# Two-layer transformer on one core: in the mixture of experts, the experts' shares come by DMA from scratch memory instead of by a matmul

## The chip, the cores and the metric

The kernel runs on one core of one Trainium2 chip. The metric is the device time of one execution in microseconds (us). A core has five engines that run their own instruction streams and wait for one another on semaphores: PE (TensorE, the matrix engine; its weight loads are listed apart as PEld), DVE (VectorE), ACT (ScalarE), POOL (GpSimd) and SP, which here only issues DMAs. PE writes its results to PSUM, eight banks of 512 fp32 values for each of 128 partitions; DVE and ACT read and write PSUM and SBUF; POOL and the DMAs don't reach PSUM.

## The reference, cut to what matters

The program computes two transformer layers on 4096 tokens of width 256. The change touches only the last part, the mixture of experts of layer 1:

```python
probs = softmax(xf @ router_w + router_b)          # 64 experts
tw, ti = top_k(probs, 8);  tw = tw / sum(tw)
for e in experts:                                   # hidden width 64 each
    h = silu(xf @ W1[e] + B1[e]) @ W2[e] + B2[e]
    cw = sum(where(ti == e, tw, 0))                 # the expert's share of each token
    acc += cw[:, None] * h
shared = sum over 2 shared experts of silu(xf @ sw1 + sb1) @ sw2 + sb2   # hidden width 512 each
out = x + acc + shared
```

All 64 experts are computed for all tokens; a token's share of an expert is zero unless the expert is among its best 8. The share is multiplied into the expert's hidden layer, before the second product.

## The kernel before

`moe_blocks` works on 8 blocks of 512 tokens, with features on the partitions and tokens along the free axis. A block has 40 chunks of 128 hidden rows: chunks 0 to 7 are the shared experts, chunks 8 to 39 are 32 pairs of experts with 64 rows each. Every fp32 product is made of three matmuls of rounded halves (hi by hi, hi by lo, lo by hi; the helper `product3`, lines 67 to 69), so a chunk's first layer is 6 matmuls into `m_h` ("hidden") and its second layer 6 more that accumulate into `m_y` ("output"). PE's order is written out by hand: hidden(c), then output(c-2) (`LAG` is 2), then hidden(c+1), and so on. Between hidden(c) and output(c) the chunk passes through ACT and DVE:

- ACT, line 1939: Silu with bias, from `m_h` in PSUM to `m_h_full` in SBUF
- DVE, line 2042, expert chunks only: multiply by the share, which is in `m_c` in PSUM
- ACT, line 1945: round to `m_h_hi`
- DVE, line 2045: subtract, to `m_h_lo`

The shares come from the router. At the start of a block PE makes the logits (into `m_turn`), DVE and ACT make the softmax and the best 8 between chunks 0 and 6, PE transposes the 64 by 512 shares after chunk 7 (line 1911), and DVE cuts them into `cw`, 64 rows of hi parts above 64 rows of lo parts (lines 2030 and 2032). A row of `cw` is one expert, but a chunk needs the row of expert 2p on 64 partitions and that of expert 2p+1 on the other 64. PE spreads them: a matmul of `cw` with a 0/1 matrix `pick_pair` (line 1852), which POOL writes for each pair (line 1826). This matmul stands in PE's order right behind hidden(c), and waits for `cw` in the block's first expert chunk:

```python
project3(nc, h_ps[:, c % 2, :], w, ln.cut[0], cols).then_inc(h_done, 1)
if c >= SC:
    ...
    nc.tensor.matmul(c_ps[:, c % 2, :], pick_pair[...], cw[:, :], start=True, stop=True).then_inc(spread, 1)
```

Among the chunks lies other work: in chunks 12 to 22 the LayerNorm of the next block (PE's two sums, lines 143 and 150; ACT's square root with two table loads, line 185, ahead of chunk 18; DVE's reciprocal in two halves behind chunks 19 and 21, line 165, and its scaling behind 22, line 170). In block 0 the experts' weights are also split into hi and lo, one item in each of 18 chunks (ACT line 991, DVE line 996). Behind a block's chunk 2 PE transposes the finished block before it into `m_c` (line 1881) and ACT copies it out in two instructions (line 1951).

PSUM is full: `m_turn`, `m_h`, `m_c` and `m_y` have two banks each. `m_h_full`, `m_h_hi` and `m_h_lo` have a ring of three places.

Of the kernel before, what the change touches and what calls it, by code (L numbers as in the profile page):

```python
# [112 lines left out]
def count(events):  # L113


    return events + FIRST
# [1605 lines left out]
HEAD = 3  # L1722


def moe_blocks(nc, d, K, w1, w2, s1, s2, rw, items):
# [7 lines left out]
    with ExitStack() as ctx:  # L1733
# [4 lines left out]
        h_full = sb("m_h_full", [P, RING, TB], F32)  # L1738
        h = [sb(f"m_h_{p}", [P, RING, TB], F32R) for p in ("hi", "lo")]
        best, row_max, row_sum = sb("best", [P, TT, TOP], F32), sb("row_max", [P, TT], F32), sb("row_sum", [P, TT], F32)  # L1740
        cw = sb("cw", [P, TB], F32R)
        pick = sb("pick", [P, E], F32)
        pick_pair = sb("pick_pair", [P, 2, 2, EH], F32R)
# [3 lines left out]
        turn_ps, h_ps, c_ps, y_ps = (ps(n, [P, 2, TB]) for n in ("m_turn", "m_h", "m_c", "m_y"))  # L1747
        (bias_loaded, pick_set, b_cut, x_loaded, x_reloaded, logit_done, logit_ready, max_ready,
         cent_ready, exp_ready, best_ready, drop_ready, kept_ready, sum_ready, r_ready, cw_ready, cw_turned,
         cw_hi, cw_lo, h_done, spread, full_ready, hi_ready, lo_ready, h_free, x4_ready, out_turned,  # L1750
         out_ready, out_stored, kept_weights, picked, dve_passed, pe_passed, passed) = (
            sem(n) for n in (
                "bias_loaded", "pick", "b_cut", "x_loaded", "x_reloaded", "logit_done",
                "logit_ready", "max", "cent", "exp", "best", "drop", "kept", "sum", "r", "cw", "cw_turned",
                "cw_hi", "cw_lo", "h_done", "spread", "full", "hi", "lo", "h_free", "x4", "out_turned",
                "out_ready", "out_stored", "kept_weights", "picked", "dve_passed", "pe_passed",
                "pool_passed"))
        sp_passed = sem("sp_passed")
        ln = LayerNorm("ln4", nc, sb, sem, K["ones"], [x], x_loaded, turn_ps[:, 0, :], turn_ps[:, 1, :])

        logits, dropped = (ln.xc[:, k, 0:TT * E].rearrange("p (t e) -> p t e", t=TT) for k in range(2))
        b2_raw = h_full[:, 2, 0:D]
# [12 lines left out]
        def heads_and_tails(eng, head, tail):  # L1775

            head(0, False)
            tail(0, True)
            head(1, True)
            with eng.Fori(1, NB - 1) as i:  # L1780
                tail(i, True)
                head(i + 1, True)
            tail(NB - 1, False)

        sem.start()
        with nc.Block() as block:
# [25 lines left out]
            @block.gpsimd  # L1812
            def _(pool):

                nc.gpsimd.memset(pick[:, :], 0.0).then_inc(pick_set, 1)
                for n, base in enumerate((0, -E)):
                    pool.wait_ge(pick_set, count(n + 1))
                    nc.gpsimd.affine_select(out=pick[:, :], in_=pick[:, :], compare_op=ALU.not_equal,
                                            fill=1.0, base=base, pattern=[[-1, E]],
                                            channel_multiplier=1).then_inc(pick_set, 1)  # L1820
                pool.wait_ge(pick_set, count(3))
                with pool.Fori(0, NB) as i:
                    for p in range(PAIRS):
                        pool.wait_ge(spread, count(i * PAIRS + max(p - 1, 0)))
                        alone(pool, passed)
                        nc.gpsimd.tensor_copy(pick_pair[:, p % 2, :, :],
                                              pick[:, 2 * p:2 * p + 2].unsqueeze(2).to_broadcast([P, 2, EH])
                                              ).then_inc(picked, 1)
                        pool.wait_ge(picked, count(i * PAIRS + (p + 1)))

            @block.tensor
            def _(pe):
                def hidden(i, c):
                    pe.wait_ge(full_ready, count(i * C + max(c - 1, 0)))
# [8 lines left out]
                    project3(nc, h_ps[:, c % 2, :], w, ln.cut[0], cols).then_inc(h_done, 1)  # L1843
                    if c >= SC:
# [310 lines left out]
```

## Time and profile before

| what | value |
|---|---|
| median of 3 runs | 4845.29 us (4844.75 to 4852.0) |
| the profiled execution | 4846.32 us, of which the span from first to last instruction is 4844.7 us |
| mean granted TensorE clock | 0.962 of full speed |
| busy over the span | PE 93%, PEld 56%, DVE 75%, ACT 65%, POOL 11% |
| the mixture of experts | its first matmul starts at 3793.8 us; 8 blocks of about 126 us each |

A matmul's listed duration contains its way through the pipeline, and matmuls overlap: for the pace of PE, the distance between starts is to be read, not the duration. A number in brackets behind a row of the timeline is how long the engine sat idle ahead of it, and what ended that. In a line that groups instructions, the first numbers are the busy time and the mean of one.

### The profile page before, as it was taken

Reading aid. Unit: us, or ns where it says so; the run is one execution under the profiler, and the core shown is the slowest. Engines: PE = TensorE matmul, PEld = TensorE weight load, DVE = VectorE, ACT = ScalarE, POOL = GpSimd, SP = SyncE. Lnnn points to the kernel's source line nnn. Section 1 sums busy time; section 2 is a strip of 40 time slices with the busy share of each in tenths; the row PEclk is TensorE's granted clock in tenths of the full one; section 3 lists DMA queues with packets and bytes.
Section 4 is the critical chain, followed back from the end, with each engine's and each line's share of the span. In section 5 each row is a group of like instructions: output and inputs, shape, how many; then the busy total and the mean of one; then the engine's idle time right before and its main releaser. Section 6 shows DMA issues by size and latency. Waiting matters only on the chain. (4 is left out here: it accounts for less than half of the span.)

```text
span 4844.7 us, 107645 instructions
## 1 busy us (share of the span) xinstructions
PE 4509.8 (93%) x36227; PEld 2729.0 (56%) x36227; DVE 3645.8 (75%) x3699; ACT 3157.8 (65%) x5605; POOL 541.7 (11%) x1382
## 2 busy tenths in 40 slices
PE   6599999999999999999999969999885799999999
PEld 4344444444444444444444447777654478888887
DVE  4599999899999999999999956555355554444444
ACT  3158888788888888888888834444464454444444
POOL 4501111111111111111111100000000000000000
PEclk8789999999999999999999979999998899999999
DMA  5611110200202012012122220010001300000000
GB/s 174 190 29 21 24 28 18 34 18 18 34 18 34 19 21 35 18 31 65 39 56 45 44 88 28 25 35 9 27 17 48 123 14 9 13 13 13 13 4 14
DMA packets 217985, 182.41 MB, mean 38 GB/s; under 512 B 128032, under 2 KB 167632, under 8 KB 216448
## 3 DMA queue, kind: packets, MB, share of 16 engines
q1 hardware_dynamic: 201152, 167.99, 14.0%
q0 software_dynamic: 16384, 8.42, 0.7%
q8 instruction: 283, 4.64, 0.4%
q14 instruction: 166, 1.36, 0.1%
HBM read 120.47 MB, written 71.89 MB: 40 GB/s over the span
## 5 line engine op out<-in xcount | busy, mean ns | idle before, releaser
L894 DVE TENSOR_REDUCE PM<-A 128x2 f32<-128x1024 f32 x2092 | 2457.2, 1220 | 97.3 <-PE A L781 64.9
L871 ACT ACTIVATE PR<-SB 128x512 f32<-128x512 f32 x4100 | 2121.1, 603 | 367.2 <-PE SB L794 354.6
L814 PE MATMUL PV<-PR,VH 128*32 128x256 f32 x16384 | 1293.4, 387 | 3.5 <-issue 3.5
L781 PE MATMUL A<-QST,KA 48*128 48x512 f32 x4184 | 1196.4, 476 | 67.0 <-DMA QF<-QFD 40.8
L814 PEld LDWEIGHTS PV<-PR,VH 128*32 128x32 f32 x16384 | 433.2, 110 | 557.9 <-issue 367.0
L781 PEld LDWEIGHTS A<-QST,KA 48*128 48x128 f32 x4184 | 428.7, 187 | 525.1 <-issue 457.8
L794 PE MATMUL SB<-KST,QST 50*128 50x512 f32 x3075 | 689.8, 411 | 5.1 <-ACT PR L871 4.6
L794 PEld LDWEIGHTS SB<-KST,QST 50*128 50x128 f32 x3075 | 387.9, 187 | 213.3 <-ACT PR L871 209.3
L2045 DVE TENSOR_TENSOR m_h_lo<-m_h_full,m_h_hi 128x512 fp32r<-128x512 f32 x320 | 221.6, 693 | 276.5 <-ACT m_h_hi L1945 276.2
L802 PE MATMUL SB<-KF,QF 99*32 99x512 bf16 x4100 | 414.9, 384 | 1.2 <-ACT PR L871 1.2
L1939 ACT ACTIVATE m_h_full<-m_h,constants 128x512 f32<-128x512 f32 x320 | 219.6, 686 | 255.4 <-PE m_h L69 254.2
L1945 ACT CAST m_h_hi<-m_h_full 128x512 fp32r<-128x512 f32 x320 | 198.6, 621 | 249.9 <-DVE m_h_full L2042 247.9
L2042 DVE TENSOR_TENSOR m_h_full<-m_h_full,m_c 128x512 f32<-128x512 f32 x256 | 175.0, 684 | 217.8 <-ACT m_h_full L1939 190.3
L1247 DVE SCALAR_TENSOR_TENSOR chosen<-gate_out,h_ps 128x512 f32<-128x512 f32 x128 | 87.1, 681 | 182.1 <-PE h_ps L69 181.7
L953 POOL DMA_DIRECT2D NUM<-OS x256 | 126.7, 495 | 864.1 <-ACT OS L882 800.6
L1186 ACT ACTIVATE h_full<-chosen,constants 128x512 f32<-128x512 f32 x128 | 92.3, 721 | 198.4 <-DVE chosen L1247 198.4
L67 PE MATMUL m_h<-ln_hi,moe_w_hi 128*128 128x512 f32 x512 | 209.0, 408 | 0.0
L67 PE MATMUL m_y<-m_h_hi,moe_w_hi 128*128 128x512 f32 x512 | 201.5, 393 | 1.8 <-DVE m_h_lo L2045 1.8
L68 PE MATMUL m_h<-ln_lo,moe_w_hi 128*128 128x512 f32 x512 | 202.6, 396 | 0.0
L69 PE MATMUL m_h<-ln_hi,moe_w_lo 128*128 128x512 f32 x512 | 202.1, 395 | 0.0
L68 PE MATMUL m_y<-m_h_lo,moe_w_hi 128*128 128x512 f32 x512 | 202.0, 394 | 0.0
L69 PE MATMUL m_y<-m_h_hi,moe_w_lo 128*128 128x512 f32 x512 | 199.7, 390 | 0.0
(280 smaller groups left out, 5503.6 us busy)
## 6 DMA issues: line engine op xcount, KB each, us to landing
QST<-QS SPq DMA_DIRECT2D x54, 256.0 KB, 9.0
KA<-KAD SPq DMA_DIRECT2D x402, 32.0 KB, 1.8
KST<-KS SPq DMA_DIRECT2D x402, 32.0 KB, 1.9
QS<-parts SPq DMA_DIRECT2D x16, 512.0 KB, 5.6
KS<-parts SPq DMA_DIRECT2D x16, 512.0 KB, 4.7
KAD<-dealt SPq DMA_DIRECT2D x16, 512.0 KB, 3.3
m_x<-X3T SPq DMA_DIRECT2D x16, 512.0 KB, 3.8
moe_w_lo<-W SPq DMA_DIRECT2D x16, 512.0 KB, 10.0
```

The costliest lines, as they stand in the source:

```text
L67: nc.tensor.matmul(out, w[0], x[0], start=first, stop=False)
L68: nc.tensor.matmul(out, w[0], x[1], start=False, stop=False)
L69: return nc.tensor.matmul(out, w[1], x[0], start=False, stop=last)
L781: return nc.tensor.matmul(A[:, u % 2 * 2 + e, :], keys, QST[rows, slot, j * TB:(j + 1) * TB], start=True, stop=True)
L794: nc.tensor.matmul(SB[:, s_bank(v), :], QST[rows, slot, c * P:(c + 1) * P], KST[rows, nb % K_SLOTS, :], start=True, stop=True).then_inc(s_ ...
L802: mm = nc.tensor.matmul(SB[r * 2 * HD:(r + 1) * 2 * HD, s_bank(v), :], QF[0:FINE_ROWS, slot, at:at + 2 * HD], KF[0:FINE_ROWS, nb % K_SLOTS ...
L814: mm = nc.tensor.matmul(PV[at:at + 2 * HD, 0:HB], VH[:, slot, e, c, :], PR[:, (2 * c + e) % P_SLOTS, b * HB:(b + 1) * HB], start=(c == 0), ...
L871: nc.scalar.activation(PR[:, v % P_SLOTS, :], SB[:, s_bank(v), :], ACT.Exp, scale=SCALE).then_inc(s_free, 1)
L894: nc.vector.tensor_reduce(PM[:, par, :, i, j:j + 1], A[:, u % 2 * 2:u % 2 * 2 + 2, :], AX.X, ALU.max).then_inc(a_free, 1)
L1939: nc.scalar.activation(h_full[:, c % RING, :], h_ps[:, c % 2, :], ACT.Silu, bias=bias).then_inc(full_ready, 1)
L1945: nc.scalar.copy(h[0][:, c % RING, :], h_full[:, c % RING, :]).then_inc(hi_ready, 1)
L2045: nc.vector.tensor_tensor(h[1][:, c % RING, :], h_full[:, c % RING, :], h[0][:, c % RING, :].bitcast(F32), ALU.subtract).then_inc(lo_ready, 1)
```

## The change

The matmul of line 1852, `m_c`, `pick` and `pick_pair` go. DVE copies the transposed shares once more, as fp32, into `m_shares` in SBUF. POOL stores them to scratch memory (`CW`, 64 by 512, fp32, 128 KB), waits for that store, and then issues two DMAs for each pair: row 2p of `CW` to all of partitions 0 to 63 of a slot of `m_shares`, and row 2p+1 to partitions 64 to 127 (128 KB written each). There are three slots; the loads of pair p wait until DVE has multiplied pair p-3. DVE waits for a pair's two DMAs and multiplies.

The two banks of `m_c` are given out anew: `m_h` has three banks, and the transposes of the finished block have one, `m_out`, so these are done and copied out in two halves (behind chunk 2 and in chunk 3). ACT's Silu and DVE's multiplication now write their result back to `m_h` in PSUM, and the two splits read it there; `m_h_full` is gone. The router's steps on DVE and ACT, and PE's transposes of the shares, each come one chunk earlier. PE's wait for `cw` moves to the products with the second bias at the block's end.

```diff
             def _(pool):
-                nc.gpsimd.memset(pick[:, :], 0.0).then_inc(pick_set, 1)
...
                 with pool.Fori(0, NB) as i:
+                    pool.wait_ge(cw_full, count(i + 1))
+                    alone(pool, passed)
+                    pool.dma_start(d["CW"], shares[0:E, 0, :]).then_inc(shares_stored, 16)
+                    pool.wait_ge(shares_stored, i * 16 + 16)
+                    alone(pool, passed)
                     for p in range(PAIRS):
-                        pool.wait_ge(spread, count(i * PAIRS + max(p - 1, 0)))
-                        alone(pool, passed)
-                        nc.gpsimd.tensor_copy(pick_pair[:, p % 2, :, :],
...
+                        if p >= SHARE_SLOTS:
+                            pool.wait_ge(kept_ready, count(i * PAIRS + (p - SHARE_SLOTS + 1)))
+                            alone(pool, passed)
+                        for e in range(2):
+                            pool.dma_start(shares[e * EH:(e + 1) * EH, p % SHARE_SLOTS, :],
+                                           d["CW"][2 * p + e, :].partition_broadcast(EH)
+                                           ).then_inc(share_loaded[p % SHARE_SLOTS], 16)
...
                 def hidden(i, c):
-                    pe.wait_ge(full_ready, count(i * C + max(c - 1, 0)))
+                    pe.wait_ge(lo_ready, count(i * C + max(c - 2, 0)))
...
-                    project3(nc, h_ps[:, c % 2, :], w, ln.cut[0], cols).then_inc(h_done, 1)
-                    if c >= SC:
...
-                        nc.tensor.matmul(c_ps[:, c % 2, :],
...
+                    project3(nc, h_ps[:, c % RING, :], w, ln.cut[0], cols).then_inc(h_done, 1)
...
-                    nc.scalar.activation(h_full[:, c % RING, :], h_ps[:, c % 2, :], ACT.Silu,
+                    nc.scalar.activation(h_ps[:, c % RING, :], h_ps[:, c % RING, :], ACT.Silu,
                                          bias=bias).then_inc(full_ready, 1)
...
-                    nc.scalar.copy(h[0][:, c % RING, :], h_full[:, c % RING, :]).then_inc(hi_ready, 1)
+                    nc.scalar.copy(h[0][:, c % RING, :], h_ps[:, c % RING, :]).then_inc(hi_ready, 1)
...
                     elif step == "cut":
                         dve.wait_ge(cw_turned, count(i + 1))
+                        nc.vector.tensor_copy(shares[0:E, 0, :], turn_ps[0:E, 1, :]).then_inc(cw_full, 1)
...
-                        dve.wait_ge(spread, count(i * PAIRS + (c - SC + 1)))
-                        nc.vector.tensor_tensor(h_full[:, c % RING, :], h_full[:, c % RING, :], c_ps[:, c % 2, :],
+                        slot, turn = (c - SC) % SHARE_SLOTS, (c - SC) // SHARE_SLOTS
+                        turns = len(range(slot, PAIRS, SHARE_SLOTS))
+                        dve.wait_ge(share_loaded[slot], i * (32 * turns) + 32 * (turn + 1))
+                        nc.vector.tensor_tensor(h_ps[:, c % RING, :], h_ps[:, c % RING, :], shares[:, slot, :],
                                                 ALU.mult).then_inc(kept_ready, 1)
...
-                        router(i, {4: "best", 5: "drop", 6: "weights", 7: "cut"}.get(c))
+                        router(i, {3: "best", 4: "drop", 5: "weights", 6: "cut"}.get(c))
```

On PE, where the shared chunks end and the expert chunks begin in block 0, `m_y` being the second layer, `m_h` the first, and line 1911 the transposes of the shares:

```order
 L68 MATMUL m_y<-m_h_lo,moe_s_hi 128x512
 L69 MATMUL m_y<-m_h_hi,moe_s_lo 128x512
-L1911 MATMUL m_turn<-ident,ln_xc 64x128 x4
-L67 MATMUL m_h<-ln_hi,moe_w_hi 128x512
-L68 MATMUL m_h<-ln_lo,moe_w_hi 128x512
-L69 MATMUL m_h<-ln_hi,moe_w_lo 128x512
-L67 MATMUL m_h<-ln_hi,moe_w_hi 128x512
-L68 MATMUL m_h<-ln_lo,moe_w_hi 128x512
-L69 MATMUL m_h<-ln_hi,moe_w_lo 128x512
-L1852 MATMUL m_c<-cw,pick_pair 128x512
```

The transposes have moved up by one chunk (they stand ahead of hidden(7) now), and behind hidden(8), as behind each later expert chunk, the matmul of line 1852 is gone; the six of hidden stand there as before.

On DVE, at the same place of block 0, before (line 996 is a weight's split, lines 2020 and 2024 the router's step "weights", lines 2030 and 2032 the step "cut"):

```order
L2045 TENSOR_TENSOR m_h_lo<-m_h_full,m_h_hi 128x512
L2020 TENSOR_TENSOR ln_xc<-ln_xc 128x256
L2024 TENSOR_TENSOR ln_xc<-ln_xc,row_sum 128x256
L996 TENSOR_TENSOR moe_w_lo<-moe_w_lo,moe_w_hi 128x1024
L2045 TENSOR_TENSOR m_h_lo<-m_h_full,m_h_hi 128x512
L2030 CAST cw<-m_turn 64x512
L2032 TENSOR_TENSOR cw<-m_turn,cw 64x512
L2042 TENSOR_TENSOR m_h_full<-m_h_full,m_c 128x512
```

and now:

```order
L2020 TENSOR_TENSOR ln_xc<-ln_xc,row_sum 128x256
L2044 TENSOR_TENSOR m_h_lo<-m_h,m_h_hi 128x512
L2025 COPY m_shares<-m_turn 64x512
L2027 CAST cw<-m_turn 64x512
L2029 TENSOR_TENSOR cw<-m_turn,cw 64x512
L996 TENSOR_TENSOR moe_w_lo<-moe_w_lo,moe_w_hi 128x1024
L2044 TENSOR_TENSOR m_h_lo<-m_h,m_h_hi 128x512
L2041 TENSOR_TENSOR m_h<-m_h,m_shares 128x512
```

The copy to `m_shares` is ahead of the cut, and chunk 7's last step (the second line 2044) now lies between the cut and the first multiplication.

On POOL, the start of a block, where ahead of the change each row was a write of `pick_pair` (line 1826):

```order
L1817 ISA
L1820 DMA CW<-m_shares 64x512
L1821 ISA
L1828 DMA m_shares<-CW 64x512 x6
L1825 ISA
L1828 DMA m_shares<-CW 64x512 x2
```

The store is followed by the six loads of pairs 0 to 2 without a wait among them, and then by two loads for each further pair.

## Rows read from the trace of the kernel before

**Rows 1.** Busy time by stretch, one block of the mixture of experts (PE first)

```profile
core 0: us, PE busy (x) PEld busy (x) DVE busy (x) ACT busy (x) POOL busy (x), PEclk, DMA share, GB/s
4593.00:4716.00 123.00, 122.48 (x541) 98.45 (x540) 59.90 (x96) 57.14 (x85) 10.46 (x32) 1.00 0.04 13
```

**Rows 2.** Groups by line, the whole mixture of experts

```profile
L1852 PE MATMUL m_c<-cw,pick_pair 128*128 128x512 f32 x256 | 101.2, 395 | 4.6 <-DVE cw L2032 4.4 <-DVE m_h_full L2042 0.2
```

**Rows 3.** What PE waited for there: us in total, times, longest

```profile
PE m_c L1852 <- DVE cw L2032: 4.4, 8, 1.0
PE m_y L67 <- DVE m_h_lo L2045: 1.8, 3, 1.0
```

**Rows 4.** Timeline, the steady pace: the last two expert chunks of a block

```profile
4449.00 0.39 PE L1852 MATMUL m_c<-cw,pick_pair 128*128 128x512 f32 x1
...
4451.77 0.39 PE L69 MATMUL m_h<-ln_hi,moe_w_lo 128*128 128x512 f32 x1
4452.00 0.39 PE L1852 MATMUL m_c<-cw,pick_pair 128*128 128x512 f32 x1
4452.20 0.69 ACT L1939 ACTIVATE m_h_full<-m_h,constants 128x512 f32<-128x512 f32 x1 [0.85 <-PE m_h L69]
...
4453.01 0.69 DVE L2042 TENSOR_TENSOR m_h_full<-m_h_full,m_c 128x512 f32<-128x512 f32 x1 [0.94 <-ACT m_h_full L1939]
...
4453.73 0.62 ACT L1945 CAST m_h_hi<-m_h_full 128x512 fp32r<-128x512 f32 x1 [0.84 <-DVE m_h_full L2042]
...
4454.39 0.69 DVE L2045 TENSOR_TENSOR m_h_lo<-m_h_full,m_h_hi 128x512 fp32r<-128x512 f32 x1 [0.69 <-ACT m_h_hi L1945]
...
4455.93 0.39 PE L67 MATMUL m_y<-m_h_hi,moe_w_hi 128*128 128x512 f32 x1
```

**Rows 5.** Timeline, chunks 18 to 23 of a block, with the next block's LayerNorm

```profile
4515.85 1.28 ACT L185 ACT_TABLE_LOAD   x1
...
4516.26 0.39 PE L69 MATMUL m_h<-ln_hi,moe_w_lo 128*128 128x512 f32 x1
...
4519.15 0.69 ACT L1939 ACTIVATE m_h_full<-m_h,constants 128x512 f32<-128x512 f32 x1
...
4519.96 0.69 DVE L2042 TENSOR_TENSOR m_h_full<-m_h_full,m_c 128x512 f32<-128x512 f32 x1 [3.40 <-PE m_c L1852]
...
4534.35 0.68 DVE L2042 TENSOR_TENSOR m_h_full<-m_h_full,m_c 128x512 f32<-128x512 f32 x1
```

**Rows 6.** Group by line: the weights' splits on DVE in block 0

```profile
L996 DVE TENSOR_TENSOR moe_w_lo<-moe_w_lo,moe_w_hi 128x1024 fp32r<-128x1024 f32 x16 | 19.7, 1230 | 6.6 <-ACT moe_w_hi L991 6.6
```

**Rows 7.** Timeline, chunks 7 and 8 of a block, with the shares' way

```profile
4478.74 0.40 PE L69 MATMUL m_h<-ln_hi,moe_s_lo 128*128 128x512 f32 x1
...
4480.72 0.48 PE L67 MATMUL m_h<-ln_hi,moe_w_hi 128*128 128x512 f32 x1
...
4481.16 0.68 DVE L2030 CAST cw<-m_turn 64x512 fp32r<-64x512 f32 x1
...
4481.96 0.40 PE L69 MATMUL m_h<-ln_hi,moe_w_lo 128*128 128x512 f32 x1
...
4482.87 0.49 PE L1852 MATMUL m_c<-cw,pick_pair 128*128 128x512 f32 x1 [0.52 <-DVE cw L2032]
```

**Rows 8.** DMA issues by kind: count, KB each, median us from issue to landing

```profile
NUM<-OS POOLq DMA_DIRECT2D x256, 16.0 KB, 2.0
out<-ln_sq SPq DMA_DIRECT2D x8, 512.0 KB, 3.0
constants<-in_L_attn_b_qkv SPq DMA_DIRECT2D x1, 128.0 KB, 4.6
```

**Rows 9.** DMA rate in 0.1 us slices of 2546 to 2550 us

```profile
GB/s 0 0 0 0 0 0 0 0 0 103 164 225 185 195 123 113 10 0 0 20 0 0 0 72 51 31 21 0 0 82 0 0 0 0 0 0 0 0 0 0
```

**Rows 10.** Timeline of POOL, two of eight DMAs (16 partitions of 1 KB each)

```profile
2785.30 0.48 POOL L953 DMA_DIRECT2D NUM<-OS  x1
2785.78 0.48 POOL L953 DMA_DIRECT2D DEN<-OS  x1
```

**Rows 11.** Groups by line: the same two splits with a PSUM source

```profile
L287 ACT CAST wt_hi<-setup_ps 128x512 fp32r<-128x512 f32 x8 | 4.4, 593 | 10.0 <-PE setup_ps L268 9.9
L298 DVE TENSOR_TENSOR wt_lo<-setup_ps,wt_hi 128x512 fp32r<-128x512 f32 x8 | 5.1, 683 | 12.9 <-ACT wt_hi L287 12.9
```

More of the change, by code:

```diff
@@ L1906, in tail @@
                         output(i, c - LAG)
-                        if c == SC - 1:
+                        if finish and c == HEAD:
+                            turn_output(i - 1, 1)
+                        if c == SC - 2:
                             pe.wait_ge(cw_ready, count(i + 1))
@@ L1927, in _ @@
                 heads_and_tails(pe, head, tail)
-                turn_output(NB - 1)
+                for part in range(2):
+                    turn_output(NB - 1, part)
             @block.scalar
@@ L1944, in chunk, with copy_output @@
                         act.wait_ge(kept_ready, count(i * PAIRS + (c - SC + 1)))
-                    nc.scalar.copy(h[0][:, c % RING, :], h_full[:, c % RING, :]).then_inc(hi_ready, 1)
-                def copy_output(i):
-                    act.wait_ge(out_turned, count(i + 1))
-                    for t in range(2):
-                        nc.scalar.copy(out_tok[:, 2 * t:2 * t + 2, :],
-                                       c_ps[:, t, :].rearrange("p (a n) -> p a n", a=2)).then_inc(out_ready, 1)
+                    nc.scalar.copy(h[0][:, c % RING, :], h_ps[:, c % RING, :]).then_inc(hi_ready, 1)
+                def copy_output(i, part):
+                    act.wait_ge(out_turned, count(i * 2 + (part + 1)))
+                    nc.scalar.copy(out_tok[:, 2 * part:2 * part + 2, :],
+                                   out_ps[:, :].rearrange("p (a n) -> p a n", a=2)).then_inc(out_ready, 1)
                 def head(i, finish):
@@ L1957, in head, with tail @@
                     if finish:
[L1958 to L1960 removed]
+                        copy_output(i - 1, 0)
+                def tail(i, following, finish):
                     for c in range(HEAD, C):
[L1962 removed]
+                        if finish and c == HEAD + 1:
+                            copy_output(i - 1, 1)
+                        if c == HEAD:
                             act.wait_ge(cent_ready, count(i + 1))
@@ L1984, in _ @@
                 heads_and_tails(act, head, tail)
-                copy_output(NB - 1)
+                for part in range(2):
+                    copy_output(NB - 1, part)
             @block.vector
```

76 lines of the change are left out of this document (30 added, 46 removed).

## The prediction, made before the changed kernel was run

> **What bounds the kernel now.** I read the table of stretches first. One block of the mixture of experts takes some 123 us, and in it PE is busy for all but half a microsecond, at the full clock of 2.4 GHz (granted clock 1.00), while DVE and ACT are busy for half of it [rows 1]. What PE waited for in the whole part is small too: 4.4 us for the shares, once in each block, and 1.8 us for the split hidden layer [rows 3]. So this part is bound by the number of PE's instructions, and one matmul less in its stream should be worth its distance to the next. The timeline gives that distance: from the matmul of line 1852 in one chunk to that in the next are 3.00 us for 13 matmuls, 0.231 us each [rows 4] (the group's mean of 395 ns holds the pipeline as well [rows 2]).
>
> The second thing to read is how late the ACT and DVE steps may be. In a chunk without other work the last matmul of hidden starts at 4451.77, Silu 0.43 later, the multiplication 0.81 after that, the rounding 0.72, the subtraction 0.66, and it takes 0.69: the chunk is ready 3.31 us after the start of that matmul [rows 4]. PE comes back for it after output(c-2), hidden(c+1), output(c-1), hidden(c+2) and three matmuls of line 1852, 28 starts later: 6.47 us. The slack is 3.1 us, and it is what now hides everything that DVE and ACT do beside the chunks.
>
> **The matmuls that go.** There are 256 of line 1852 [rows 2], at 0.231 us: 59.2 us, if nothing takes their place.
>
> **The wait that goes.** In the first expert chunk PE starts its last matmul of hidden at 4481.96 and that of line 1852 only at 4482.87, 0.91 us later instead of 0.23: 0.68 us, of which 0.52 are shown as idle [rows 7]. With the same 0.16 us beside the idle time in all 8 blocks the 4.4 us [rows 3] become 5.7 us. The new reader of `cw`, the bias at the block's end, comes 80 us later and never waits.
>
> **The slack that shrinks.** The chunk's period falls to 12 × 0.231 = 2.77 us. PE comes back for a chunk after 25 starts, 5.77 us. The reads from PSUM change the two splits a little: rounding takes 593 ns from PSUM [rows 11] against 0.62, the subtraction 683 ns [rows 11] against 0.69. What it costs or gives to write the Silu and the product to PSUM no row shows, since nothing but PE writes there before. I bound it by what the source does, 0.03 us better or worse for each, take nothing, and get 3.27 us from matmul to ready chunk, and some 0.1 for the wake-up: 2.4 us of slack. The Trainium skill ("ScalarE: Activation LUTs", Step-by-step: what each stage is for) says that ACT writes faster to PSUM than to SBUF; by it the Silu would fall towards the lower bound and some of the stalls below would go. No run here shows it yet.
>
> Where is the slack used up? At chunk 18 ACT is held by two table loads and the square root from 4515.85, and its Silu starts at 4519.15. Now hidden(18) is complete in time for a start at 4516.26 + 0.43 = 4516.69, 2.46 us earlier [rows 5], inside the 3.1. With the new pace that matmul comes 0.23 us sooner, while ACT's work behind chunk 17 does not: 2.67 us late, over the slack by 0.27. From there to chunk 23 DVE has the reciprocal twice and the scaling as well: multiplication to multiplication 4519.96 to 4534.35, 14.39 us for 5 chunks [rows 5], 14.2 with the quicker splits. PE's five periods are 5 × 3.00 = 15.0 now, so the chain catches up; they will be 13.87, so it falls behind by another 0.33. PE is stalled by 0.27 + 0.33 = 0.6 us in each of the 6 blocks between the first and last: 3.6 us. Block 0 has the weights' splits in addition, 1.2 us of DVE each [rows 6]. From chunk 18 to 28 the chain needs 11 × 2.05 (its own minimum, 0.81 to the multiplication, 0.72 to the rounding and 0.52 until ACT takes the next Silu) + 7 × 1.2 for the splits there + 3.3 for the square root (4515.85 to 4519.15) + 4.1 for reciprocals and scaling (14.39 less 5 × 2.05 [rows 5]) = 38.4 us. PE needs 33.0 for 11 chunks now, and 38.4 - 33.0 - 3.1 = 2.3 is near the 1.8 us plus wake-ups that the trace has [rows 3]. With 30.5 and 2.4 it gives 5.5, so 3.2 more; 2.8 with the quicker splits.
>
> **The shares' new way.** Take as zero the start of the last matmul of hidden in the chunk ahead of the transposes: 7 before, 6 now. DVE began the cut 2.42 us later (4478.74 to 4481.16) and takes 0.68 [rows 7]. The new copy comes first and has that form: ready at 3.1. POOL needs about 0.15 to start. Its store of 128 KB lies between POOL's 16 KB in 2.0 us and 512 KB in 3.0 us [rows 8]; I take 2.3, as the size is near the small end. At 5.7 the first load is issued, at 6.2 the second: POOL's DMAs follow one another by 0.48 us [rows 10], though each has 16 rows there and 64 here. A load needs the 2.0 of a small one and the time for its bytes. For that the best row is the only large broadcast that travels alone: 128 KB, one 1 KB row to 128 partitions, 4.6 us to landing, most of it behind a copy on its queue [rows 8]. Its bytes moved in seven or eight slices of 0.1 us at 103 to 225 GB/s [rows 9], 0.8 us. Two such are 1.6 us, so pair 0 lands at 6.2 - 0.5 + 2.0 + 1.6 = 9.3 us.
>
> When is it needed? PE goes on with output(4) and the transposes until 1.98 (the distance to 4480.72 [rows 7]), then hidden(7), output(5), hidden(8), output(6), hidden(9), output(7), hidden(10), and wants chunk 8 at 11.8. The multiplication stands 2.07 us ahead of the chunk's end (4453.01 to 4455.08 [rows 4]), so it may start as late as 9.6. The landing is just in time; I take 0.3 us a block for the wake-ups, 2.4 us. Bounds: with 2.0 for each DMA the shares land at 7.9 and nothing is lost; with a store of 3.0, loads of 4.6 and an issue of 4 × 0.48 us (if it goes by rows) they land at 12.9, 3.3 us late in each block, 26 us. What waits behind that multiplication is all of DVE, then ACT's rounding, and PE at output(8). The DVE copy itself, 0.68 us, lies in the shared chunks' slack. In the steady state the loads of pair p are issued after multiplication p-3, 7.6 us ahead of their use against some 4 that they need. POOL has nothing else, and no long transfers run beside them but the 512 KB of `x`, twice a block.
>
> **The end.** The last block's output is turned and copied in two halves that wait for one another (one bank): one copy of 0.6 us is no longer hidden. 0.6 us.
>
> **The sum**, against the profiled execution's 4846.3 us: -59.2 - 5.7 + 3.6 + 2.8 + 2.4 + 0.6 = -55.5, that is 4790.8. That execution is 1.0 us over the median of the runs, so I predict 4790 us.
>
> **The rivals.**
>
> *The loads can't keep the pace, and the kernel is slower.* The place is DVE's wait for `share_loaded` in every pair. A pair has 2.77 us. If its two DMAs need R, 32 × 8 = 256 pairs lose R - 2.77 each, and the 55.5 us are gone at R = 2.99: 1.5 us of POOL for each issue, or 88 GB/s. For it: the 0.48 us [rows 10] are for 16 rows, and with 64 rows in proportion it is 1.92, R = 3.84 and the time 4790 + 256 × 1.07 = 5064 us. Against: much of such an issue should not depend on the rows, since SP's 512 KB with 128 rows and more are not slower to land than 3.0 us [rows 8]. I give this 9%. A second form of it is that all 64 partitions read the same 2 KB of memory, and the memory gives it out slowly. Against it stands the one broadcast in the trace, which moved at 160 GB/s from 1 KB [rows 9]; 2%. The Trainium skill ("SBUF — State Buffer", A bandwidth-pool intuition that's wrong) gives 22.5 GB/s for one of the 32 ports to the memory. An estimate from it, if a row sat behind one port, is 5.8 us for 128 KB, and the kernel would be over 2000 us slower; the trace disagrees, its row went out seven times as fast.
>
> *The shares are late at each block's start*, by more than I took: at 1.5 to 3.3 us in each of 8 blocks, 4800 to 4815 us. For it: every DMA in the chain is an estimate, and there are two in series. 14%.
>
> *The ACT and DVE chain becomes the bound in the LayerNorm's stretch*, if writing to PSUM is 0.03 us slower in each step or the wake-ups grow: 0.3 us more in each block and some in block 0, 4793 to 4800; this is inside the forecast's own range. *No change*: only if the gain is eaten by a near-bound load rate, 3%.
>
> **The numbers.** The forecast has 72%, with a range of its own of 4782 (no stalls at all, writes to PSUM quicker) to 4800. Late shares 14%, slower 11%, no change 3%. Two in ten may be left out: the range goes from 4780 to 4816, which takes in the late shares and leaves out the loads that can't keep pace. About 0.2%, 10 us, is what a measurement of this kernel can tell from no change. Faster 86%, same 3%, slower 11%.
>
> **What would show it.** The profile after should have PE starts of a chunk 2.77 us apart and no `m_c`; the wait of PE for `cw` gone; new waits of `m_y` for `m_h_lo` of some 6 us about chunks 18 to 23 and in block 0; DVE's multiplication of chunk 8 waiting for a DMA, with PE behind it idle for under 0.5 us. POOL's issue should last well under 1.38 us. The prediction is wrong if DVE waits for DMA in the middle of a block, if POOL is busy for the whole of it, or if the first pair lands over 10 us after hidden(6).

## The result and the profile after

The changed kernel takes 4795.14 us (median of 4 runs, 4787.88 to 4803.14) against 4845.02 (4841.52 to 4852.0): ratio 0.9891, 95% interval 0.9879 to 0.9904. The forecast was 4790, range 4780 to 4816. The gain is 1.1% and clear of the noise. The medians lie 49.9 us apart where the sum of the forecast had 55.5; the four runs of the changed kernel alone spread over 15 us, so being 5 us off the median says little for or against the sum.

The profiled execution took 4787.88 us, span 4786.3. The code ahead of this part is the same in all kernels here, and its executions reach the part's first matmul (line 143 into `m_turn`) anywhere from 3787.6 to 3804.7 us in the traces below, so all that follows is measured from that start to the span's end, "the part": 1050.9 us before (3793.8 to 4844.7), 997.9 after (3788.4 to 4786.3). The part is 53.0 us shorter; the other 5.4 of this pair of executions are not the change's.

Busy time in a block, as in [rows 1]:

```profile
core 0: us, PE busy (x) PEld busy (x) DVE busy (x) ACT busy (x) POOL busy (x), PEclk, DMA share, GB/s
4540.00:4660.00 120.00, 119.87 (x528) 95.43 (x527) 62.51 (x101) 57.83 (x90) 33.52 (x65) 1.00 0.26 84
```

PE is still busy for all of it at the full clock. POOL went from 10 to 34 us, far from a bound. (The stretch of 123 us in [rows 1] is not quite a block: from hidden(0) to the next hidden(0) a middle block takes 127.7 us before and 120.4 to 120.8 after.) What PE and DVE waited for in the part, as in [rows 3] (us in total, times, longest):

```profile
PE m_y L67 <- DVE m_h_lo L2044: 5.5, 8, 1.7
PE m_turn L1904 <- DVE ln_xc L2020: 1.5, 1, 1.5
...
DVE m_h L2041 <- DMA m_shares<-CW: 34.3, 8, 4.6
```

`cw` is gone from the list; `m_h_lo` has risen from 1.8 to 5.5: 4.8 of that is in block 0, the rest at chunk 8 of blocks 1 and 3. In the LayerNorm's stretch of the other blocks PE only starts some matmuls late, without an idle time that this list counts. DVE waits for a load 8 times, once in each block, and never in the middle of one. The steady pace, as in [rows 4]:

```profile
4403.47 0.40 PE L69 MATMUL m_h<-ln_hi,moe_w_lo 128*128 128x512 f32 x1
...
4403.90 0.66 ACT L1933 ACTIVATE m_h<-m_h,constants 128x512 f32<-128x512 f32 x1 [0.68 <-PE m_h L69]
...
4404.68 0.70 DVE L2041 TENSOR_TENSOR m_h<-m_h,m_shares 128x512 f32<-128x512 f32 x1 [0.74 <-ACT m_h L1933]
...
4405.42 0.59 ACT L1939 CAST m_h_hi<-m_h 128x512 fp32r<-128x512 f32 x1 [0.85 <-DVE m_h L2041]
...
4406.04 0.69 DVE L2044 TENSOR_TENSOR m_h_lo<-m_h,m_h_hi 128x512 fp32r<-128x512 f32 x1 [0.65 <-ACT m_h_hi L1939]
...
4406.25 0.40 PE L69 MATMUL m_h<-ln_hi,moe_w_lo 128*128 128x512 f32 x1
```

A chunk in 2.78 us, and 3.26 us from matmul to ready chunk (4403.47 to 4406.04 + 0.69; forecast 3.27). The way of the shares, as in [rows 7]:

```profile
4318.03 0.40 PE L69 MATMUL m_h<-ln_hi,moe_s_lo 128*128 128x512 f32 x1
...
4319.65 0.60 PE L1904 MATMUL m_turn<-ident,ln_xc 128*64 128x128 f32 x4
...
4319.77 0.69 DVE L2044 TENSOR_TENSOR m_h_lo<-m_h,m_h_hi 128x512 fp32r<-128x512 f32 x1 [1.23 <-ACT m_h_hi L1939]
4320.38 0.68 DVE L2025 COPY m_shares<-m_turn 64x512 f32<-64x512 f32 x1
...
4321.65 0.53 POOL L1820 DMA_DIRECT2D CW<-m_shares  x1 [30.96 <-DVE m_shares L2025]
...
4324.45 3.08 POOL L1828 DMA_DIRECT2D m_shares<-CW  x6 [2.28 <-DMA CW<-m_shares]
...
4328.00 0.70 DVE L2041 TENSOR_TENSOR m_h<-m_h,m_shares 128x512 f32<-128x512 f32 x1 [4.33 <-DMA m_shares<-CW]
...
4329.59 0.40 PE L69 MATMUL m_h<-ln_hi,moe_w_lo 128*128 128x512 f32 x1
...
4330.10 0.51 PE L67 MATMUL m_y<-m_h_hi,moe_w_hi 128*128 128x512 f32 x1
```

The first pair's multiplication starts 9.97 us behind hidden(6)'s last matmul (its second load landed 0.02 before); PE starts output(8) 0.51 after the matmul ahead of it, 0.28 late. This is block 4. In blocks 1 to 7 the multiplication starts 9.83 to 10.28 us behind hidden(6), in block 0 11.63, since the transposes are 1.5 us late there. The second load of the pair landed at 11.53 in block 0, 10.26 in block 1 and 10.10 in block 3, over the 10 us that the prediction had named as a sign of being wrong; what that costs PE is read below (e3). Groups and DMA issues, as in [rows 8, 10]:

```profile
L1828 POOL DMA_DIRECT2D m_shares<-CW x512 | 263.9, 521 | 449.0 <-DVE m_h L2041 418.1 <-DMA CW<-m_shares 18.2 <-issue 12.7
L1933 ACT ACTIVATE m_h<-m_h,constants 128x512 f32<-128x512 f32 x320 | 212.5, 664 | 207.0 <-PE m_h L69 205.1
L1939 ACT CAST m_h_hi<-m_h 128x512 fp32r<-128x512 f32 x320 | 188.0, 587 | 269.4 <-DVE m_h L2041 267.4
L2041 DVE TENSOR_TENSOR m_h<-m_h,m_shares 128x512 f32<-128x512 f32 x256 | 178.3, 697 | 180.2 <-ACT m_h L1933 145.0 <-DMA m_shares<-CW 34.3 <-issue 0.3
...
m_shares<-CW POOLq DMA_DIRECT2D x512, 128.0 KB, 2.8
```

POOL issues a load in 0.52 us with 64 rows as against 0.48 with 16, and the load lands after 2.8.

### The profile page after: what moved, and what is told of

It reads as the page before. It is cut to its first block and busy times, and to the rows that moved or that the text cites. A ratio compares the mean times of both kernels' runs of the same rounds, so it can differ in the third digit from the quotient of the medians.

```text
span 4786.3 us, 107146 instructions
## 1 busy us (share of the span) xinstructions
PE 4450.8 (93%) x35971; PEld 2675.8 (56%) x35971; DVE 3649.5 (76%) x3707; ACT 3136.7 (66%) x5605; POOL 724.8 (15%) x1643
## 5 line engine op out<-in xcount | busy, mean ns | idle before, releaser
L2044 DVE TENSOR_TENSOR m_h_lo<-m_h,m_h_hi 128x512 fp32r<-128x512 f32 x320 | 221.3, 692 | 257.3 <-ACT m_h_hi L1939 257.3
L1939 ACT CAST m_h_hi<-m_h 128x512 fp32r<-128x512 f32 x320 | 188.0, 587 | 269.4 <-DVE m_h L2041 267.4
L1933 ACT ACTIVATE m_h<-m_h,constants 128x512 f32<-128x512 f32 x320 | 212.5, 664 | 207.0 <-PE m_h L69 205.1
L1828 POOL DMA_DIRECT2D m_shares<-CW x512 | 263.9, 521 | 449.0 <-DVE m_h L2041 418.1
L2041 DVE TENSOR_TENSOR m_h<-m_h,m_shares 128x512 f32<-128x512 f32 x256 | 178.3, 697 | 180.2 <-ACT m_h L1933 145.0
L925 POOL CAST NM<-neg 128x8 fp32r<-128x8 f32 x65 | 12.3, 189 | 1300.7 <-DVE neg L901 1300.7
```

The source lines that it names most:

```text
L1828: pool.dma_start(shares[e * EH:(e + 1) * EH, p % SHARE_SLOTS, :], d["CW"][2 * p + e, :].partition_broadcast(EH)).then_inc(share_loaded[p % ...
L1933: nc.scalar.activation(h_ps[:, c % RING, :], h_ps[:, c % RING, :], ACT.Silu, bias=bias).then_inc(full_ready, 1)
L2044: nc.vector.tensor_tensor(h[1][:, c % RING, :], h_ps[:, c % RING, :], h[0][:, c % RING, :].bitcast(F32), ALU.subtract).then_inc(lo_ready, 1)
```

## The experiments

The times are the part's, each of one profiled execution. Two things move by themselves. The changed kernel gave 997.9 and, run again, 997.4 us. And behind the last block's hidden(39) there are 14.1 to 14.3 us in some executions (the changed kernel both times, e2, e9) and 13.7 in the others (e1, e3, e4, e7, e8, e10, e11) though the instructions there are the same: TensorE's clock falls in the last stretch of the program, ahead of the last four transposes or behind them. The changed kernel and e3, in the columns of the table of stretches:

```profile
4780.00:4782.00 2.00, 1.08 (x4) 0.71 (x4) 0.00 (x0) 0.78 (x2) 0.00 (x0) 0.52 0.00 0
4778.00:4779.90 1.90, 0.85 (x7) 0.42 (x4) 0.00 (x0) 0.88 (x2) 0.00 (x0) 1.00 0.00 0
```

The four transposes take 1.08 us at a granted clock of 0.52, and 0.63 in e3, where the clock was still 1.00. So 0.5 us of any difference to 997.9 can be this, and small differences are read from stretches between hidden's last matmuls instead.

**The router one chunk later (e1), in the changed kernel:**

```diff
-                        if c == SC - 2:
+                        if c == SC - 1:
-                        router(i, {3: "best", 4: "drop", 5: "weights", 6: "cut"}.get(c))
+                        router(i, {4: "best", 5: "drop", 6: "weights", 7: "cut"}.get(c))
```

> The changed kernel with the router's steps and the transposes of the shares put back by one chunk, as they stood before. All numbers are the time from the part's first matmul (line 143 into m_turn) to the span's end: 1050.9 us before, 997.9 after. My theory (the first pair's landing sets a block's chunk 8; in the profile after it comes 9.97 us behind the start of hidden(6)'s last matmul and leaves PE idle for 0.3 us): the landing moves back by one chunk, 2.78 us, and PE stalls for about 3.1 us in each block, so 997.9 + 8 x 2.8 = 1020 us. Rival 1 (the landing is not what PE waits for; the 0.3 us is wake-up or the cut's load on DVE): the time stays within 2 us of 997.9. Rival 2 (part of the lost time is won back, because chunks 9 and 10 are then already prepared): between 1005 and 1015.

Measured: 1026.5 us (3787.6 to 4814.1), 28.6 more.

```profile
PE m_y L67 <- DVE m_h_lo L2044: 28.2, 12, 3.7
```

The wait grew by 22.7 us, and at chunk 8 PE is idle for 2.75 to 3.67 in every block: the landing is what chunk 8 waits for, and my theory holds for the stall. Most of what is above the forecast's 1020 is TensorE's clock. Stretches around chunk 8 of block 1, where PE stood still for 3.17 us up to 3972.8:

```profile
3969.00:3972.80 3.80, 0.64 (x3) 0.19 (x1) 1.43 (x3) 1.15 (x2) 2.12 (x5) 1.00 0.49 180
3972.80:3977.00 4.20, 4.19 (x12) 3.28 (x13) 2.61 (x4) 1.74 (x3) 2.27 (x5) 0.61 0.43 125
3977.00:3982.00 5.00, 5.00 (x22) 3.94 (x21) 2.09 (x3) 2.25 (x4) 1.03 (x2) 0.98 0.30 89
```

After the idle time the granted clock is 0.61 (most starts are 0.43 us apart, as at 1.2 GHz), and full again some 4 us later. It fell in 5 of the 8 blocks, after idle times of 2.90 to 3.67 us, and not in the three with 2.75 to 2.93. From hidden(7) to hidden(15) middle blocks take 27.4 to 27.6 us where it did not fall and 29.1 to 30.4 where it did; less the longer idle times, I estimate some 8 us for the five falls. (Block 0's transposes no longer wait 1.5 us, and the end is 0.5 shorter.) I had not priced the clock.

**No store and no loads (e3):**

```diff
-                            pool.dma_start(shares[e * EH:(e + 1) * EH, p % SHARE_SLOTS, :], ...
+                nc.gpsimd.memset(shares[:, :, :], 0.5).then_inc(shares_set, 1)
-                        dve.wait_ge(share_loaded[slot], i * (32 * turns) + 32 * (turn + 1))
```

> The changed kernel without the store and the 64 loads of the shares in each block: POOL fills the three slots with 0.5 once, DVE multiplies by that without waiting, everything else stays. It leaves out the experts' true shares (every expert gets 0.5). Measured again from the part's first matmul to the span's end (997.9 after). My theory: the loads cost only where chunk 8 waits for the first of them, 2.4 us in all 8 blocks and 0.1 for each wake-up, so about 994.7, and the stalls of m_y in block 0 and at chunks 18 to 23 (6.7 us) stay. Rival (the loads' 64 MB also slow something else, such as PE's weight loads, the reads of SBUF or the `x` and weights' transfers): under 992 us, and the stalls in block 0 shrink.

Measured: 992.5 us, 5.4 less, between the two forecasts. PE's wait for `m_h_lo` is 4.1 us in 4 times, all of it in block 0: the same four (0.4, 0.8, 1.2 and 1.7 us) as with the loads. From hidden(7) to hidden(15) a middle block takes 23.97 us against 24.21 to 24.64 after. Summed over 8 blocks that is 3.2 us for chunk 8: I undersized it by 0.1 us a block. Block 0 gives 0.8 more, where a wait of 0.47 us at chunk 14 is gone, the LayerNorm's stretch 0.13 in each of 6 blocks, and 0.5 lie behind hidden(39), which is the clock and not the loads. So the rival has a small part: 1.6 us outside chunk 8 go with the loads, spread over 7 blocks. By what way the loads cost them was not tested; nothing that they slow is worth a us in one place.

The stretches also say when the shares are needed. In each of blocks 1 to 7 the changed kernel's is longer than e3's by what its multiplication starts behind 9.60 us (10.28 and 0.67 in block 1, 9.97 and 0.37 in block 4, 9.83 and 0.24 in block 5), to 0.01 us.

**Two slots (e2) and one (e6):**

```diff
-SHARE_SLOTS = 3
+SHARE_SLOTS = 2        # e6: 1
```

> The changed kernel with two slots of m_shares instead of three, so that pair p is loaded only after the multiplication of pair p-2. From the part's first matmul to the span's end (997.9 us after). My theory (two issues of 0.52 us follow the multiplication of p-2, and the landing is 2.8 us behind the issue: 0.7 + 0.1 + 1.04 + 2.8 = 4.6 us from the start of multiplication p-2 to the landing, against two periods of 2.77 = 5.5): the loads keep the pace with 0.9 us to spare, the time stays at 997 to 999 us, and the median landing stays at 2.8 us. Rival (the loads' rate is near its limit, and the third slot hides a queue of them): DVE waits for a DMA in most pairs, and the time rises by 50 us or more.

Measured: 1006.6 us, 8.7 more. The loads keep pace with the chunk in the sense that nothing piles up, but the slack is thinner than I said: DVE waits for a load 60 times, not 8, 75.2 us instead of 34.3. PE's wait for `m_h_lo` is 8.3 us (13 times) instead of 5.5, mostly in block 0, where DVE runs behind and a catch-up needs shares sooner; block 0 is 2.1 us longer. At the end of each of blocks 1 to 7 DVE waits 1.2 to 1.9 us for the loads of chunk 39, and PE, which comes back for it with less work between, starts late by up to 0.4 us: 1.3 us in all. Some 5 us are the clock again, which fell at the starts of three blocks (2, 3 and 7). In the middle stretch of these three most matmuls of hidden start 0.43 us apart:

```profile
4066.00:4072.50 6.50, 6.38 (x40) 5.19 (x39) 4.02 (x5) 1.53 (x2) 0.00 (x0) 1.00 0.00 1
4072.50:4076.30 3.80, 3.80 (x12) 3.00 (x12) 0.00 (x0) 0.97 (x2) 0.00 (x0) 0.55 0.00 0
4076.30:4082.00 5.70, 5.70 (x28) 4.66 (x27) 3.22 (x6) 4.32 (x7) 0.00 (x0) 1.00 0.00 0
```

Ahead of it PE was idle for 0.1 us only and then ran the 24 short matmuls of the logits (64 columns). Why it fell here and not in the changed kernel stays open, and with one execution it is not shown that the two slots are its cause. So both theories missed: no rate limit, and, without the clock, some 4 us for the third slot.

> The changed kernel with a single slot: pair p is loaded only after the multiplication of pair p-1, so that a pair's period is the loop of multiplication, two issues, landing, wake-up. It measures that loop. From the part's first matmul to the span's end (997.9 us after). My theory (0.70 for the multiplication, 0.1 + 1.04 for the two issues, 2.8 for the landing, 0.1 for the wake-up: 4.7 us for each of 32 pairs, where the pace was 2.77): 31 x 8 x 1.9 = 480 us more, about 1480. Rival (each load has its bytes' time only, and issue and landing overlap in part): 4.0 us or less a pair, 1300 us or less. A load that takes over 5.5 us alone would give 1680 or more and would mean that two loads in flight are what keeps the pace.

Measured: 1507.4 us, 509.5 more, 2.05 for each of 248 pairs. The loop:

```profile
4613.05 0.70 DVE L2041 TENSOR_TENSOR m_h<-m_h,m_shares 128x512 f32<-128x512 f32 x1 [2.73 <-DMA m_shares<-CW]
...
4617.85 0.70 DVE L2041 TENSOR_TENSOR m_h<-m_h,m_shares 128x512 f32<-128x512 f32 x1 [2.76 <-DMA m_shares<-CW]
```

```profile
4614.32 1.04 POOL L1828 DMA_DIRECT2D m_shares<-CW  x2 [3.74 <-DVE m_h L2041]
```

4.80 us (forecast 4.7): 0.70 for the multiplication, 0.57 until POOL starts, 1.04 for two issues, 2.49 to the next multiplication. That 4.7 was so near is partly luck: I had taken 0.1 for POOL's start, 0.47 too little, and 2.8 + 0.1 from the end of the two issues, though the 2.8 us of a landing count from the start of an issue, 0.4 too much. Over all pairs the multiplications of a block are 4.79 us apart on average (2.84 with three slots), 485 of the 509.5 us. The other 24 lie between the blocks, where the clock is at its lower level for up to 17 us at a time.

**Hidden layer in SBUF (e4):**

```diff
-                    nc.scalar.activation(h_ps[:, c % RING, :], h_ps[:, c % RING, :], ACT.Silu,
+                    nc.scalar.activation(h[1][:, c % RING, :], h_ps[:, c % RING, :], ACT.Silu,
```

and the same for the product and the sources of the two splits.

> The changed kernel with the Silu, its product and the splits' source in SBUF again (in the place of m_h_lo, in place, so that the hidden layer is already rounded there and its lo part is mostly lost; the instructions are as many and as large). From the part's first matmul to the span's end (997.9 after). My theory (PSUM or SBUF matters by hundredths of a us for each step: 3.26 us from matmul to ready chunk after, 3.31 before): the steady pace stays at 2.77 us a chunk, the stalls in block 0 and at chunks 18 to 23 grow by some 0.15 us x 6 and 1 us, so 998.5 to 1001. Rival (writing to PSUM is what keeps the chain inside PE's shorter period): chain 3.4 us or more, more than 1003 us.

Measured: 999.3 us, 1.4 more, as my theory had it.

```profile
L1933 ACT ACTIVATE m_h_lo<-m_h,constants 128x512 fp32r<-128x512 f32 x320 | 219.5, 686 | 194.7 <-PE m_h L69 193.6
L1939 ACT CAST m_h_hi<-m_h_lo 128x512 fp32r<-128x512 f32 x320 | 198.7, 621 | 265.2 <-DVE m_h_lo L2042 263.2
L2042 DVE TENSOR_TENSOR m_h_lo<-m_h_lo,m_shares 128x512 fp32r<-128x512 f32 x256 | 175.9, 687 | 174.7 <-ACT m_h_lo L1933 140.0 <-DMA m_shares<-CW 33.7 <-issue 0.3
```

PSUM gives 22 and 34 ns on ACT and takes 10 on DVE. (The types of the outputs differ too; but the kernel before, with fp32 outputs in SBUF, has 686, 621 and 684.) Block 0 is 1.0 us longer and the LayerNorm's stretch 0.15 in each of 6 blocks, as forecast. Its use in the change is mostly another: `m_shares` has the size of `m_h_full`, which it replaces.

**The kernel before, router one chunk earlier (e5):**

```diff
-                        if c == SC - 1:
+                        if c == SC - 2:
-                        router(i, {4: "best", 5: "drop", 6: "weights", 7: "cut"}.get(c))
+                        router(i, {3: "best", 4: "drop", 5: "weights", 6: "cut"}.get(c))
```

> The kernel before, with its matmul that spreads the shares, and only the router's steps and the transposes of the shares one chunk earlier, as the change has them. From the part's first matmul to the span's end (1050.9 before). My theory: the 4.4 us of wait for cw and 0.16 us beside each go, and nothing else moves: 1045 to 1046 us, so this part of the gain needs no DMA. Rival (DVE's cut and chunk 7's last step collide and chunk 7's output waits instead, or block 0's splits move): 1048 us or more.

Measured: 1046.3 us, 4.6 less. The wait for `cw` is gone; middle blocks gain 0.8 us each, but block 0 loses 0.6, as PE's transposes now wait 1.5 us there for the router's weights (0.4 before).

**Splits elsewhere (e7), and the router yet one chunk earlier with them (e8):**

```diff
-        CUTS = {..., 7: (10,), 10: (11,), 11: (12,), 12: (13,), 15: (14,), 18: (15,), 19: (16,), 20: (17,), 23: (18,), 26: (19,), ...
+        CUTS = {..., 7: (10,), 8: (11,), 9: (12,), 10: (13,), 12: (14,), 14: (15,), 16: (16,), 24: (17,), 25: (18,), 27: (19,), ...
```

```diff
-                        if c == SC - 2:
+                        if c == SC - 3:
```

> The changed kernel with another table of the chunks of block 0 in which a weight is split: none from chunk 17 to 23, where DVE and ACT have the next block's LayerNorm; some come up to 4 chunks earlier, the others 1 to 6 later. As many splits. From the part's first matmul to the span's end (997.9 us after). My theory (block 0's stalls of m_y, 5.6 us in the starts of PE's matmuls, come from the split beside the LayerNorm's steps): 3.5 to 5 us less, 993 to 994.5. Rival (the sum of DVE's and ACT's work in block 0 is what PE waits for, wherever it stands, or the early splits come ahead of the weights' transfers): no less than 996 us, with the stalls at other chunks.

> The same table of splits, and in addition the router's steps again one chunk earlier: the transposes of the shares behind hidden(5), best and drop in one chunk, then the weights, then the cut. From the part's first matmul to the span's end (997.9 us after). My theory: the stalls at each block's chunk 8 (2.4 us in all, and 0.1 behind each) go as well, and block 0's wait of the transposes for the router's weights grows by up to 1 us: 990 to 993 us. Rival 1 (the router's steps can't come earlier, since ACT and DVE are behind at a block's start: PE's transposes wait for the weights in every block): 997 us or more. Rival 2 (it is not the first load's landing that chunk 8 waits for): equal to the kernel with the table alone.

Measured: 996.0 and 998.2. With the table alone 1.9 us went, 1.4 of them in block 0 and 0.5 at the end, where it is the clock. The waits at chunks 18 to 23 (4.1 us) are gone, but new ones stand at chunks 9, 10, 24 and 25 of block 0 (0.4 us each), and the one at 14 has grown from 0.5 to 1.0; each of the five chunks has a split in the new table. So the rival is nearly right: the stalls mostly moved. In e8 chunk 8's stalls are gone in blocks 1 to 7, but PE's transposes wait instead:

```profile
PE m_turn L1904 <- DVE ln_xc L2020: 5.5, 8, 2.8
```

2.8 us in block 0 and 0.39 in each other block: the first rival. (Behind the 2.81 us of idle time in block 0 the clock fell once more.) The router can't come a whole chunk earlier.

**The transposes 0.69 us earlier, between the halves of output(4) (e9):**

```diff
+                        if between and n == 0:
+                            between()
```

> The changed kernel with the four transposes of the shares moved ahead by three matmuls, 0.69 us, to between the two halves of output(4). In the profile after, the weights of the router are ready at 4318.54 in a block, the first half of output(4) ends its issue at 4318.96, so PE need not wait; in block 0 the weights come 1.5 us late already. From the part's first matmul to the span's end (997.9 us after). My theory (the way transposes, copy, store, load to chunk 8 is one chain, and moves as a whole): the stalls of 0.2 to 0.4 us at chunk 8 go in blocks 1 to 7, in all 2 to 3 us, and block 0 is unchanged: 995 to 996 us. Rival (the copy on DVE stands behind chunk 6's last step and does not start sooner, or PE waits at the transposes instead, as it did with a whole chunk): 997.5 us or more.

Measured: 997.6 us. The theory fell. PE turned the shares at 4451.12 without waiting, but DVE copied them no sooner:

```profile
4451.94 0.69 DVE L2047 TENSOR_TENSOR m_h_lo<-m_h,m_h_hi 128x512 fp32r<-128x512 f32 x1 [1.21 <-ACT m_h_hi L1942]
4452.55 0.67 DVE L2028 COPY m_shares<-m_turn 64x512 f32<-64x512 f32 x1
```

Line 2047 is chunk 6's subtraction, ahead of the copy in DVE's order, and it waits for hidden(6). The copy starts 2.36 us behind hidden(6)'s last matmul (4450.19); in the changed kernel it is 2.35. What starts the shares' way is chunk 6's own chain. A copy put ahead of that subtraction was not tried.

**LayerNorm later (e10), and all three (e11):**

```diff
-                        if following and c in (19, 21):
+                        if following and c in (20, 22):
-                        if following and c == 22:
+                        if following and c == 25:
```

In e11: square root ahead of chunk 30, reciprocals behind 32 and 34, scaling behind 36, the transposes as in e9, and splits in chunks 16 to 28.

> The changed kernel with the next block's reciprocals behind chunks 20 and 22 instead of 19 and 21, and the scaling behind 25 instead of 22. From the part's first matmul to the span's end (997.9 us after). My theory: the lag at chunk 18 is 2.64 us, each chunk wins back 0.78, a reciprocal costs 1.65, the scaling 1.13, so that the lag falls to 1.1 ahead of each reciprocal, stays under 2.1 behind it, and only some 0.1 of the 0.4 us lost between chunks 18 and 23 is left: 6 x 0.3 = 2 us less, and in block 0, where splits lie among them, 1 us more or less: 995 to 997 us. Rival (the 0.4 us are not lag but the cost of reading and writing the same banks): 997.5 or more.

> The transposes between the two halves, the next block's square root ahead of chunk 30, reciprocals behind 32 and 34, scaling behind 36, and a table of splits in block 0 that uses chunks 16 to 28, free of the LayerNorm now. From the part's first matmul to the span's end (997.9 us after). My theory, by the same bookkeeping of lags: 2.5 us at chunk 8, 2.4 in the LayerNorm's stretch and 3 us in block 0 go: 989 to 992 us, and the whole kernel is 5 to 9 us faster than the changed one. Rival (the lag returns at the block's end, where PE comes back for chunks 38 and 39 after fewer matmuls): stalls of m_y there in each block, 994 us or more.

> The changed kernel once more, for a ratio with the one above on the same chip. The part should take 998 us again, within 1 us where TensorE's clock behaves alike, and the whole 4788 to 4803 us, since what comes ahead of the part has differed by up to 10 us between profiled executions of kernels that are alike there.

Measured: 995.8 for e10, 991.9 for e11, 997.4 for the changed kernel again. In e10 chunks 25 to 39 of a middle block take 39.01 us, PE's own minimum, instead of 39.29, 1.7 us over 6 blocks: the bookkeeping of lags holds. In e11 PE waits for `m_h_lo` only 2.6 us, 5 times, and block 0 is 3.1 us shorter than in the changed kernel, so the place of the splits does count once the LayerNorm's steps are out of their way. Its median is 4785.85 us (4 runs, 4780.57 to 4798.09; ratio to before 0.9876, 0.9854 to 0.9898) against 4793.04 (4782.47 to 4794.15; 0.9883, 0.9866 to 0.9899) for the changed kernel on the same chip. The part is 5.5 us shorter (0.4 of it at the end, by the clock); the whole can't tell the two apart, the intervals overlap.

## Why the prediction was right, step by step

The mechanism was right: PE's stream bounded the part, and each term of the sum is found in the runs, with its sign. The sizes were off by up to 1.9 us, and not all one way: the gains were 3.0 us too large, the costs 0.1 too large in all. The sizes come from the times between hidden's last matmuls. The router's move is e5's. Block 0 is 4.3 us shorter than in e5, where 7.2 for 32 matmuls less 0.4 at chunk 8 would give 6.8: 2.4 are lost.

| step | predicted | measured |
|---|---|---|
| the matmuls that go | -59.2 | -57.3 |
| the wait that goes, with block 0's new wait | -5.7 | -4.6 |
| the slack that shrinks, 6 blocks | +3.6 | +2.8 |
| the slack that shrinks, block 0 | +2.8 | +2.4 |
| the shares' new way | +2.4 | +3.2 |
| the end | +0.6 | +0.9 |
| sum, of 53.0 in the part | -55.5 | -52.6 |

- **The matmuls.** 14 undisturbed chunks take 42.14 us before and 39.01 after, 3.010 and 2.786 a chunk. The difference is 0.224, not 0.231: the average over 13 starts (3.010 / 13 = 0.232) is not what the thirteenth costs. Why it costs less was not tested. This is the largest error, 1.9 us.
- **The wait** was sized well where it stood (0.68 and a little behind it in a middle block). What I missed is that moving the transposes ahead leaves block 0's router late, 1.1 us there.
- **The slack.** The changed kernel's rows, as in [rows 5]:

```profile
4355.42 1.28 ACT L185 ACT_TABLE_LOAD   x1
...
4355.65 0.40 PE L69 MATMUL m_h<-ln_hi,moe_w_lo 128*128 128x512 f32 x1
...
4358.72 0.66 ACT L1933 ACTIVATE m_h<-m_h,constants 128x512 f32<-128x512 f32 x1
...
4373.65 0.69 DVE L2041 TENSOR_TENSOR m_h<-m_h,m_shares 128x512 f32<-128x512 f32 x1
...
4375.74 0.50 PE L67 MATMUL m_y<-m_h_hi,moe_w_hi 128*128 128x512 f32 x1
```

Silu of chunk 18 is 2.64 us late (4358.72 less 4355.65 + 0.43; forecast 2.67). From hidden(15) to hidden(25) and on to hidden(39) a middle block takes 29.74 and 39.29 us, where e11 has 29.56 for the first (without the LayerNorm's later steps) and e10 39.01 for the second: 0.46 us are lost, not 0.6: 0.18 up to hidden(25), which has the return for chunk 18 in it (forecast 0.27), and 0.28 behind it, where that for chunk 23 is (0.33). The mechanism is as forecast; the slack was some 0.1 larger.
- **The shares' way** landed at 9.97, forecast 9.3. Copy ready at 3.03 (3.1); POOL starts the store 0.59 later (0.15 taken); the store lands 2.24 after its issue (2.3); POOL issues the first load 0.57 after that (0.15 taken); first load's issue to use 3.55 (3.6). So the store and the load were sized well from [rows 8] and [rows 9], and what was short is POOL's start, by 0.4 us, twice. No row of the prediction shows its 0.15; the trace before has both values: a cast of POOL's starts 0.16 us behind the end of the matmul that released it (4482.87 + 0.49 in [rows 7]), a DMA 0.58 behind the end of ACT's copy:

```profile
4483.52 0.29 POOL L1826 CAST pick_pair<-pick 128x128 fp32r<-128x128 f32 x1 [30.18 <-PE m_c L1852]
...
2783.32 0.41 ACT L882 COPY OS<-PV 128x256 f32<-128x256 f32 x1
2784.31 0.52 POOL L953 DMA_DIRECT2D NUM<-OS  x1 [12.84 <-ACT OS L882]
```

The latest start, 9.6, held (e3; the 11.8 for chunk 8 is 11.7 by the prediction's own terms, and 11.7 is measured). Since the landing was forecast ahead of it, the 2.4 us were an allowance for wake-ups, and that 3.2 are near is luck in part: the 0.4 us a block are the late landing. By the prediction's own sign (over 10 us) this step failed in blocks 0, 1 and 3; it cost 0.4 to 0.7 us in each.
- **The end.** The two halves cost 0.45 us (0.6 forecast); the other 0.45 is the clock in the second set of transposes, whose four matmuls ran from 4780.50 for 1.08 us, where e3 has 0.63. Most of the executions after the change don't have it, so it is no cost of the change.
- **PSUM.** Taken as nothing; it is little: Silu 664 ns instead of 686, product 697 instead of 684. That ACT writes faster to PSUM, as the Trainium skill ("ScalarE: Activation LUTs", Step-by-step: what each stage is for) says, is borne out, by 22 ns.
- **The rivals.** *Can't keep the pace*: refuted, issue 0.52 us and not 1.92, and two rows feed 256 KB every 2.79 us, 94 GB/s. The estimate of 5.8 us for a row behind one port, from the Trainium skill ("SBUF — State Buffer", A bandwidth-pool intuition that's wrong), does not fit: 2.8 us from issue to landing. *Late shares* did not come at the size given (1.5 to 3.3 us in each block; it is 0.2 to 0.7); e1 shows what it would have cost, about one to one in idle time and more by the clock. *ACT and DVE as the bound*: only inside the stretches that the forecast had.

## What to carry to other kernels

When one instruction leaves a periodic stream, its price is the difference of two periods, and the engines that hid behind the old period must be checked against the new slack, lag by lag: the LayerNorm, the weights' splits and the shares each took back a few us here. A chain through memory (copy, store, load) starts with whatever stands ahead of its first instruction in that engine's order; moving its producer earlier gains nothing until that is out of the way. A wait's end to an engine's start is to be taken from a row of the same engine and the same kind of instruction: POOL's casts started within 0.16 us, its DMAs after 0.57 or more. Buffers beyond what the mean pace needs pay where the consumer catches up in a burst.

## What the runs showed of the hardware

POOL began a DMA 0.57 to 0.59 us after the DVE instruction that released it, a store's landing was followed by the next issue after 0.57, and in the trace before a cast of POOL's began 0.16 us after its release.

In e1 TensorE's granted clock fell to its lower level in 5 of 8 blocks, after 2.90 to 3.67 us of idle time (not after 2.75, 2.76 and, once, 2.93), and was back after some 3 to 6 us of matmuls; in e8 it fell after 2.81 us. In e2 it fell at the start of a block after 0.1 us of idle time and 24 matmuls of 64 columns. With one slot (e6) the mean granted clock was 0.947 instead of 0.962, which is part of its 509 us.
